# The second attention layer of a fused graph and expert layer: streamed attention tiles, a row of sums, side rows through TensorE and ScalarE

## What is computed

```python
def gat_conv(x, src, dst, W, a_src, a_dst, bias, H, C, n):
    h = (x @ W).reshape(n, H, C)
    s_src, s_dst = (h * a_src).sum(-1), (h * a_dst).sum(-1)
    e = leaky_relu(s_src[src] + s_dst[dst], 0.2)
    ee = exp(e - segment_max(e, dst)[dst])
    alpha = ee / segment_sum(ee, dst)[dst]
    return segment_sum(alpha[:, :, None] * h[src], dst).reshape(n, H * C) + bias

out1 = gat_conv(x_norm, ..., H=4, C=192)
out2 = gat_conv(out1, ..., H=2, C=96)
gnn = concatenate([xn, out2], -1) @ Wu + bu
x = x + gnn + mix(xn)                   # mix: linear attention
x = x + alpha * shared(xn2) + (1 - alpha) * routed_top2(xn2)
```

## Time and profile before

| | us |
|---|---|
| Median of three runs | 1594.6 (1594.26 to 1594.98) |
| The profiled execution | 1598.5 |
| Its span in the trace | 1596.8 |
| TensorE busy | 1524.4 (95%) |
| VectorE busy | 824.9 (52%) |
| ScalarE busy | 329.6 (21%) |
| GpSimd busy | 450.4 (28%) |

### The profile page before, as it was taken

One profiled execution on the slowest core, in us unless ns is written; L12 is line 12 of the kernel. 1 busy time (PEld: TensorE's weight loads), 2 busy tenths in 40 slices (PEclk: granted clock), 3 DMA queues, 4 the chain that ended last, 5 costly groups with the idle time before them and its releaser, 6 DMA issues.

```text
span 1596.8 us, 21967 instructions
## 1 busy us (share of the span) xinstructions
PE 1524.4 (95%) x8300; PEld 1001.8 (63%) x8301; DVE 824.9 (52%) x1526; ACT 329.6 (21%) x481; POOL 450.4 (28%) x466
## 2 busy tenths in 40 slices
PE   5999999999999899999989997999999999999996
PEld 3566676558889899999886554444444444444442
DVE  8655457886678799876987142212122222221221
ACT  3321121112240445640671110100000000000000
POOL 1187865653300000000000047032232333232322
PEclk9999999999999999999999999999999999999998
DMA  9900010000034427114203247915619322613451
GB/s 260 363 2 2 2 63 1 1 1 1 1 81 131 108 57 210 35 22 103 61 1 97 112 97 169 303 51 198 220 48 337 101 55 54 207 50 116 154 201 26
DMA packets 83372, 163.81 MB, mean 103 GB/s; under 512 B 19979, under 2 KB 61185, under 8 KB 80730
## 3 DMA queue, kind: packets, MB, share of 16 engines
q1 hardware_dynamic: 55383, 119.07, 23.0%
q0 software_dynamic: 12096, 23.27, 6.6%
q10 hardware_dynamic: 15810, 20.41, 5.0%
HBM read 127.75 MB, written 37.56 MB: 104 GB/s over the span
## 4 chain that ended last, share of the span: by engine, by line
PE 80%; DVE 10%; issue 3%; DMA 3%; POOL 1%; ACT 1%; SPq 0%; ACTq 0%; DVEq 0%; POOLq 0%
PE bank L828 34%; PE bank L1722 6%; PE bank L1683 6%; PE bank L1585 5%; PE bank L1498 5%; PE bank L1642 5%; PE bank L1470 4%; PE bank L738 3%; DVE arena L2453 2%; PE bank L1523 2%; DVE arena L2422 2%; DMA expert_in<-arena 2%; DVE arena L2398 2%; PE bank L1770 2%; POOL expert_in L694 1%
## 5 line engine op out<-in xcount | busy, mean ns | idle before, releaser
L828 PE MATMUL bank<-arena 128*64 128x384 f32 x3312 | 544.7, 487 | 0.6 <-ACT arena L916 0.6
L828 PEld LDWEIGHTS bank<-arena 128*64 128x64 f32 x3312 | 233.9, 137 | 287.3 <-issue 286.4
L1722 PE MATMUL bank<-arena 125*125 125x198 f32 (+1 forms) x1200 | 192.4, 321 | 12.1 <-DVE arena L2422 11.9
L1722 PEld LDWEIGHTS bank<-arena 125*125 125x125 f32 x1200 | 186.1, 196 | 16.3 <-DVE arena L2422 16.2
L1188 DVE TENSOR_TENSOR arena<-bank,arena 128x384 f32<-128x384 f32 x46 | 25.7, 558 | 302.0 <-PE bank L828 302.0
L1683 PE MATMUL bank<-arena 128*125 128x192 f32 x960 | 164.0, 329 | 0.6 <-DVE arena L2375 0.6
L1683 PEld LDWEIGHTS bank<-arena 128*125 128x125 f32 x960 | 157.7, 189 | 0.9 <-DVE arena L2375 0.9
L1376 POOL TENSOR_SCALAR arena<-arena 128x125 bf16<-128x125 f16 x186 | 115.4, 623 | 111.6 <-PE bank L1523 106.8
L1370 POOL DMA_INDIRECT slot_table<-arena x80 | 112.0, 1400 | 93.8 <-issue 93.8
L2261 DVE TENSOR_TENSOR arena<-arena,bank 125x417 f32 x186 | 109.8, 590 | 52.1 <-PE bank L1523 43.4
L717 POOL TENSOR_TENSOR arena<-arena 64x768 f32<-64x768 f32 x44 | 79.6, 1808 | 185.3 <-DMA arena<-out_dram,arena 141.6
(11 more groups left out here) (310 smaller groups left out, 1663.6 us busy)
## 6 DMA issues: line engine op xcount, KB each, us to landing
arena<-in_L_ffn_w_gate_dram SPq DMA_DIRECT2D x9, 2304.0 KB, 10.0
arena<-in_L_ffn_w_up_dram SPq DMA_DIRECT2D x9, 2304.0 KB, 10.8
arena<-in_L_ffn_w_down_dram SPq DMA_DIRECT2D x9, 2304.0 KB, 9.9
arena<-score_rows ACTq DMA_DIRECT2D x18, 585.9 KB
expert_in<-arena SPq DMA_DIRECT2D x23, 384.0 KB, 10.5
arena<-expert_in ACTq DMA_DIRECT2D x92, 96.0 KB, 2.4
...
```

Of the source, the lines that this page charges most:

```text
L828: ins = tp.matmul(ps[bank][HP * h:HP * h + HP, 0:384], frm[:, b, k, HP * h:HP * h + HP], ew[h][i][:, k, n * 384:(n + 1) * 384], start=(k = ...
L1722: ins = tp.matmul(ps[bank][0:T, c * width:(c + 1) * width], ptile[0:T, j % NPT, dt * T:(dt + 1) * T], values(n - first, st), start=(st == ...
```

## The change

In layer 2 the operands of the attention product are exchanged: the values (97 columns) become the stationary operand, and P streams past in pieces of 417, 417 and 416 columns (`OP`), so the result comes out transposed, in banks 0 to 2 for head 4 and 3 to 5 for head 5. The sums are then a row on one partition. VectorE inverts this row in three pieces (`invert_sums`), TensorE spreads each piece over 96 partitions with a product by ones (`spread_sums`), ScalarE copies it, and VectorE multiplies (`divide_head`), straight into `out2T`; `out2` and `turn_out` go. The bias is added to the values by two small matmuls into the row that is added to layer 1's result.

28 of the 32 side units behind layer 1 are completed on TensorE: a seventh matmul by the identity adds the row that VectorE added before, and ScalarE copies the result (`take_sides` of ScalarE). The tables of their places change. The score row of head 4 is spread by ten transposes into banks 0 to 2 and copied by ScalarE, instead of by way of memory. The load of head 2's score row is issued by ScalarE after the second exponential of layer 1 instead of ahead of head 0. The eight reads of the first expert rows are issued by SyncE, ahead of its load of the second expert's gate weights. The transposes of the layer's row sets use bank 4 in place of 5. The diff, cut to its core:

```diff
-        out2 = take(NT * H2 * C2).rearrange("p (t h c) -> p t h c", t=NT, h=H2)
...
-        SIDE_START2 = (3, 7, 8, 9)
+        SIDE_START2 = (2, 0, 10, 7)
 
         def side_layer2(h, st):
-            return ((0, 1, 1, 1, 0, 0, 0, 0, 0, 0), (0,) * 10)[h][st]
+            return ((0, 1, 1, 1, 1, 1, 1, 1, 1, 1), (1, 1, 0, 0, 0, 0, 0, 0, 0, 0))[h][st]
+
+        ACT_SIDES = sum(SIDE_START2[1:]) + sum(side_layer2(h, s) for h in range(H2) for s in range(NT))
+        ACT_FIRST = 2 * NF - SIDE_END - ACT_SIDES
...
-        AHEAD = 6
+        AHEAD1, AHEAD2 = 6, 8
...
-                    (0,) * 10, (0, 1, 1, 1, 1, 0, 0, 0, 0, 0), (0,) * 10)[n][st]
+                    (0,) * 10, (0, 1, 1, 0, 0, 0, 0, 0, 0, 0), (0,) * 10)[n][st]
...
+        OP = [(0, 417), (417, 417), (834, 416)]
...
+            for i in range(4):
+                sp.dma_start(xgb[32 * i:32 * i + 32, 0], xg_dram[32 * i:32 * i + 32]).then_inc(s_xg[0], 16)
+            rows = xg_dram[P:2 * P].rearrange("(i r) d -> r i d", r=32)
+            for c in range(4):
+                sp.dma_start(xgb[32 * c:32 * c + 32, 1].rearrange("p (i d) -> p i d", i=4), rows[:, :, FW * c:FW * c + FW])\
+                    .then_inc(s_xg[1], 16)
             load_expert(1, 0)
...
-                if t == 6:
-                    act.wait_ge(s_rows, 16 * 2 * NT)
-                    load_first_x()
-                    load_x(1, 1)
...
+                    by_act = 0 <= u - ACT_FIRST < ACT_SIDES
                     for k in range(KD):
                         ins = tp.matmul(ps[side_bank(u)][0:T, 0:FW], frm[:, k, t * T:(t + 1) * T], wchunk[:, c % 2, k, :],
-                                        start=(k == 0), stop=(k == KD - 1))
+                                        start=(k == 0), stop=(k == KD - 1 and not by_act))
+                    if by_act:
+                        if t == 0 or u == ACT_FIRST:
+                            pe.wait_ge(s_x[CHUNKS[c]], 64)
+                        ins = tp.matmul(ps[side_bank(u)][0:T, 0:FW], ident[0:T, 0:T], x2[0:T, t, CHUNKS[c]], start=False, stop=True)
...
+                for i, (a, m) in enumerate(OP):
+                    ins = tp.matmul(ps[3 * h + i][0:C2 + 1, 0:m], h2acc[0:T, st, h * (C2 + 1):(h + 1) * (C2 + 1)],
+                                    ptile[0:T, j % NPT, a:a + m], start=(st == 0), stop=(st == NT - 1), skip_group_check=True)
...
+            def spread_sums(h, i):
+                a, m = OP[i]
+                pe.wait_ge(s_hout, NT * H1 + 6 * h + i + 1)
+                if (h, i) == (0, 2):
+                    pe.wait_ge(s_recs, 1)
+                tp.matmul(ps[spread_bank(h, i)][0:C2, 0:m], iota[0:1, 1:2].to_broadcast([1, C2]), srowb[0:1, h, a:a + m],
+                          start=True, stop=True).then_inc(s_recb, 1)
...
+            for i, (a, m) in enumerate(PIECES):
+                for d in range(m):
+                    ins = tp.transpose(ps[i][0:T, d * T:(d + 1) * T], s2rows[0:T, a + d:a + d + 1].to_broadcast([T, T]), ident[0:T, 0:T])
+                ins.then_inc(s_spread, 1)
             turn_rows(S2, s2rows[0:T])
...
-            side_units(SIDE_END)
-            pe.wait_ge(s_o2, 3)
+            heads(H2, H1, attend_layer2, sides2, SIDE_START2)
+            pe.wait_ge(s_hout, NT * H1 + 6)
+            side_units(1)
             for i in range(3):
-                turn_out(1, i)
+                spread_sums(1, i)
+            side_units(SIDE_END - 1)
...
-                if n + 2 < H1:
+                if 0 < n < H1 - 2:
                     score_row(n + 2)
...
+                        if (n, st) == (0, 1):
+                            score_row(2)
...
+            def take_sides(n):
+                for _ in range(n):
+                    u = sides_taken[0]
+                    act.wait_ge(s_f, u + 1)
+                    if u == ACT_FIRST:
+                        act.wait_ge(s_fe, u)
+                    sc.activation(x2[0:T, u % NT, CHUNKS[u // NT]], ps[side_bank(u)][0:T, 0:FW], ACT.Copy).then_inc(s_fe, 1)
+                    sides_taken[0] = u + 1
...
+            for i, (a, m) in enumerate(PIECES):
+                act.wait_ge(s_spread, i + 1)
+                sc.activation(srowb[0:T, 0, a * T:(a + m) * T], ps[i][0:T, 0:m * T], ACT.Copy).then_inc(s_srow[0], 1)
             take_rows(S2)
-            for h in range(H2):
-                score_row(H1 + h)
-            heads(H2, H1, aside2)
+            score_row(H1 + 1)
+            heads(H2, H1, aside2, lambda i: take_sides((SIDE_START2[1] + SIDE_START2[2], SIDE_START2[3] - 1, 1)[i]))
...
+            def invert_sums(h):
+                dve.wait_ge(s_big, H1 + H2)
+                dve.wait_ge(s_ptused, NT * (H1 + h + 1))
+                for i, (a, m) in enumerate(OP):
+                    dv.reciprocal(srowb[0:1, h, a:a + m], ps[3 * h + i][C2:C2 + 1, 0:m]).then_inc(s_hout, 1)
+
+            def divide_head(h, i):
+                a, m = OP[i]
+                dve.wait_ge(s_recs, 3 * h + i + 1)
+                dv.tensor_tensor(out2T[0:C2, h, a:a + m], ps[3 * h + i][0:C2, 0:m], srowb[0:C2, h, a:a + m], ALU.mult)\
+                    .then_inc(s_hout, 1)
...
+            invert_sums(1)
+            for i in range(3):
+                divide_head(1, i)
+            taken[0] += ACT_SIDES
+            dve.wait_ge(s_fe, taken[0])
             take_sides(SIDE_END)
```

158 lines of the change are left out of this document (85 added, 73 removed).

## The result

The changed kernel takes 1614.8 us (1610.46 to 1620.09, four runs) against 1594.8 (1594.26 to 1594.98): a ratio of 1.0119, interval 1.0094 to 1.0143. That is slower, as forecast, but 2.8 us above the range. Four later comparisons ran on two chips, the first two on one and the last two on the other. In two of them the changed kernel ran again: the median of its twelve runs there is 1613.4, and that of the 70 runs of the kernel before in the four comparisons is 1597.0. The difference is therefore nearer 16 us than the first 20 (14.8 in one comparison, 17.0 in the other).

What follows compares the result with a forecast made beforehand. TensorE was taken as the bound, with 13.0 us of waiting in layer 2, and long reciprocals as deciding. Terms -3 + 17 - 3 = +11 us gave 1609 profiled, 1605.6 median; forecast 1605 us, range 1592 to 1612.

Steps and rivals of the forecast that it cites:

- Layer 2, +17: Layer 2 up to `gnn_out`: 9.8 us later at the last product, 6.6 behind it, 1 for lower clock.
- the tail: Layer 2, from the last product to `gnn_out`: 12.7 us, where before it was 6.1.
- The reciprocals: Layer 2, VectorE: 3.3 us per long reciprocal, 9.9 us per head, bounds 0.6 and 3.6 us each; the deciding term.
- The streamed product and the seventh matmul: Layer 2, TensorE: 2.17 us per streamed tile against 2.23; seventh matmul 0.33 us, 9.2 us over 28 units.
- Layer 1, -3: Layer 1's start: moving a score row's read takes 2.4 us of transfer from in front; -3 us, bounds 0 and 5.5.
- The first expert rows, -3: Shared expert and first expert tile: row reads on SyncE end TensorE's 8.15 us wait; -3 us, bounds -11 and +1.
- The cap by the down weights: First expert tile: down weights land at 1027.6, third product could start at 1033.3, so only 5.7 us can be gained.
- the conversion from profile to median: Whole kernel: the median was taken as 3.9 us below the profiled time, turning 1609 into 1605.6 us.
- A: Rival: reciprocals at VectorE's usual slope, 0.6 us each; layer 2 costs +3, total 1591.6 us; chance 0.13.
- the -6 elsewhere: Outside layer 2: the -3 us at layer 1's start and the -3 us for the first expert rows.
- B: Rival: long reciprocals, but waits in layer 1 and at the expert rows won in full; +3, 1597.6 us; chance 0.15.
- C: Rival: head 4's rows delayed by a weight load, or ScalarE bounds the steps; +5 us, 1610 us; chance 0.12.

Runs made afterwards that it cites:

- e8: The changed kernel run again unchanged, for more runs and a second profile: 1612.5 us, ratio 1.0086.
- f1: The changed kernel run once more unchanged, in a later comparison: 1613.6 us, ratio 1.0112.
- e1: The changed kernel with the eight reads of the first expert rows put back on ScalarE: 1616.8 us, ratio 1.0125.
- e4: The changed kernel with SyncE's read of the slot table put ahead of its last twelve stores: 1614.6 us, ratio 1.0117.
- e9: The changed kernel with GpSimd's 44 additions cut to 8 of 768 columns: 1612.9 us, ratio 1.0091.
- f2: The changed kernel with GpSimd's additions cut to 8 of 768 columns, as in e9, beside the changed kernel on the same chip: 1612.6 us, ratio 1.0104.
- e2: The kernel before with only the reads of the first expert rows moved to SyncE: 1595.9 us, ratio 0.9993.
- e5: The kernel before with first expert row reads on SyncE, four store groups issued by ScalarE and the slot table read early: 1597.7 us, ratio 0.9999.
- e10: The kernel before with GpSimd's additions cut to 8 of 768 columns: 1596.7 us, ratio 1.0005.
- e3: The changed kernel with the six long reciprocals replaced by plain copies: 1605.6 us, ratio 1.0049.
- e12: The changed kernel without the seventh (identity) matmul of the 28 side units: 1613.9 us, ratio 1.0095.
- e6: The kernel before with only head 4's score row spread by TensorE transposes and its side units re-placed: 1592.6 us, ratio 0.9961.
- e11: The kernel before with the edits of both e6 and e2: 1592.2 us, ratio 0.9973.

## Why the forecast was right in sign and too low

**Layer 2, +17: right.** In the first profile +16.4 between the layer's start and `gnn_out`; the seven profiles with the changed kernel's code up to there (the first, e8, f1, e1, e4, e9, f2) have a mean of 146.8 us, the four of the kernel before (the given one, e2, e5, e10) 130.7: +16.2. Step by step: TensorE's wait on the row write 2.79 (3 taken); head 4's first tile 766.8 (766.2; but the four times behind the last units, 1.3 + 1.2 + 1.4 + 1.4, make 5.3 and not the 4.3 that were added, so the terms as written give 767.2); head 4's end 810.2 (812.0), since the half clock cost 1.8 us there instead of 3.1 and a tile follows the last after 2.10 instead of 2.17; the last product starts its pair at 841.6 and ends about 846.0 (848.3); the tail 14.3 (12.7). The reciprocals were 8.0 instead of 9.9 per head, yet head 5 was only half a microsecond shorter than forecast: VectorE waited 1.86 us for ScalarE in it, and TensorE's first tile behind the stall ran at half clock. The tail was 1.6 longer although they were shorter: the last side unit stands behind the third spread, is computed at half clock in 3.84 us, and VectorE can add it only then. The prediction counted the units' additions there, not their matmuls. e3 gives the share of the reciprocals: 10.8 of the 16.4.

**The streamed product and the seventh matmul.** Six records take 2.26 us against 2.32 or 2.42 before, and the next work starts 2.10 after them; this was as worked out. The seventh matmul is 0.33 us, as said, and its sum of 9.2 weighs 6 to 7 at `gnn_out` in e12.

**Layer 1, -3: wrong.** The term took 2.4 us of transfer away from in front of head 0's rows, and the slow tile behind the wait with it. ScalarE's first `lower`, which waits for these rows, before and after:

```profile
520.21 2.56 ACT L1964 ACTIVATE arena<-arena 125x1250 f32<-125x1250 f32 x2 [10.47 <-DMA arena<-score_rows]
```

```profile
520.65 2.57 ACT L2004 ACTIVATE arena<-arena 125x1250 f32<-125x1250 f32 x2 [9.92 <-DMA arena<-score_rows]
```

All sixteen profiles of this document can be read here, six with head 2's read at its old place (the given one, e2, e5, e6, e10, e11) and ten with it moved. The mean wait is 10.6 us in the six and 10.3 in the ten: the rows came 0.3 us sooner, not 2.4. Head 0's first tile starts at 531.1 and 530.4 in the mean, layer 2 at 713.4 and 712.4: about 1 us won, where single profiles with the same code up to there lie up to 6 us apart. The 3.14 us of the earlier trace rows stand at the long end of a range down to 2.0 in the six (e10), and the ten have 2.1 to 3.1 but for one without a wait.

The slow tile was no loss that could be won either. The first profile has the tile in 3.62 us, followed by a wait of 2.75 for head 1's rows; f1 has it in 5.29, and the wait is 1.06. Their sums are 6.37 and 6.35. TensorE of f1_after_third:

```profile
529.86 5.29 PE L1733 MATMUL bank<-arena 125*125 125x198 f32 x20 [2.30 <-DVE arena L2489]
...
548.78 0.27 PE L1639 MATMUL bank<-arena 125*20 125x125 f32 x1 [1.06 <-DVE arena L2438]
```

VectorE's rows set the pace there, and what TensorE gains is waited out at the next one. It even comes back worse: behind the longer wait the tile at 549.1 takes 4.94 us instead of 3.51, and from the first tile to the start of layer 2 it is 182.8 us in the first profile and 181.3 in f1. The prediction read the wait and the slow tile and never asked what comes next.

**The first expert rows, -3: right in its path, uncertain in size.** About -4 by the first profile: 11.2 won, 5.3 waited, 1.7 lost to the clock. The cap by the down weights was there wherever SyncE read the rows, in e2, e5 and e11 too. From `gnn_out` to the last product e2 shows 2.7 us less than the kernel before and e1 3.5 or more above the changed kernel's three, but f2 has 738.0, only 1.4 below e1, and e11 takes 735.6 where e6, with ScalarE's reads, takes 734.6. The Trainium skill, Trainium Kernel Development and Optimization, section Key Constraints, says that the queues run on the same DMA engines and that issuing from several saves only issue time. e5 is in line with it: loads issued 4.3 us sooner took 3.1 longer.

**What was missing.** For the profiles, take three of the changed kernel (the first, e8, f1). Up to `gnn_out` they have a mean of 860.1, the four of the kernel before 843.3: +16.8 where -3 and +17 had 14; with all seven it is 859.4 and +16.1. From `gnn_out` to the last product: 733.1, 735.2 and 735.9, mean 734.7, against 736.8 and 737.4 for the kernel before and e10: -2.4. Behind the last product: 15.3, 19.6 and 18.0 against 15.4: +2.3 in the mean. The sum is +16.7, and the medians of the later comparisons differ by 16.4; with single profiles microseconds apart, so close an agreement is partly luck.

So three steps of the prediction failed. The first is the -3 of layer 1, of which about 1 came. The second is a tail that isn't in the sum at all: GpSimd's chain behind the last product, put at nothing, cost 2.7 and 4.3 us in two profiles of three, though e9 and f2 leave open how much of the median it makes (0.7 us by their runs). The third is the conversion from profile to median: 3.9 us were taken off, because the profiled execution of the kernel before lay that much above three runs. For the changed kernel the profiled execution lay 4.3 us below the median of its own four runs. Of the 9.2 us between the sum's 1605.6 and the measured 1614.8, this step is 8.2 and the profile's own surplus 1.0. The 70 later runs have a median of 1597.0, 1.5 below the profiled execution, so that the baseline was a part of it.

**The rivals.** A fell with the 2.73 us reciprocal; e3, whose copies take the 0.6 us that A assumed, ran in 1605.6, not 1591.6, because layer 2 keeps a loss of some six microseconds without them (A had 3) and not all of the -6 elsewhere came. B fell with layer 1 and with the 5.3 us on the down weights. Of C little was seen: head 4's first tile came when forecast, so its rows were not late, and in head 5 VectorE waited for ScalarE's `lower` once, for 1.86 us.

What stays open: why the half-clock episodes fall where they do, why e12 gained nothing in its median, what in TensorE's added work makes the rest of the layer's loss, and how much GpSimd's chain adds to the median.
